# FFN gates turned and broadcast as twelve bf16 rows instead of four fp32 rows, and register waits bounded by an AND

## The reference

```python
all_out = _experts_mlp(x, eW1, eb1, eW2, eb2, eW3, eb3)      # 4 experts, 256 -> 128 -> 64 -> 256
shared = _shared_mlp(x, sW1, sb1, sW2, sb2, sW3, sb3)
gates = jax.nn.softmax(x @ gW + gb, axis=-1)
topv, topi = jax.lax.top_k(gates, TOPK)                      # the best 2 of 4
topw = jax.nn.softmax(topv, axis=-1)
sel = jnp.take_along_axis(all_out, topi[:, :, None, :], axis=-1)
gated = jnp.sum(sel * topw[:, :, None, :], axis=-1)
return shared + gated
```

## Time and profile before

| | us |
|---|---|
| median of three runs | 1826.44 |
| lowest and highest of them | 1825.96, 1827.35 |
| span of the profiled execution, first to last instruction | 1822.0 |
| median less that span | 4.4 |
| TensorE busy, of the span | 1704.3 |
| VectorE, ScalarE, GpSimd busy | 942.9, 569.8, 186.2 |

### The profile page before, as it was taken

How to read it: one execution, slowest core, us unless ns; L and a number is a source line. 1 busy time by engine, 2 the same in 40 slices (tenths; PEclk the granted TensorE clock), 3 DMA queues, 4 the chain that set the end, 5 groups by cost and what they waited for, 6 DMA issues and landing times.

```text
span 1822.0 us, 30852 instructions
## 1 busy us (share of the span) xinstructions
PE 1704.3 (94%) x10162; PEld 1363.7 (75%) x10163; DVE 942.9 (52%) x1593; ACT 569.8 (31%) x854; POOL 186.2 (10%) x260
## 2 busy tenths in 40 slices
PE   6999999888879999999999999999999999998995
PEld 4898988888766777777777777767677777787784
DVE  7999999998862300111144443552312243245436
ACT  2135677888880100000011111343400000004442
POOL 4000000000000100000000000000000000153683
PEclk9999999999999999999999999999999999999998
DMA  4203344544569445454443435900054434434375
GB/s 98 1 34 124 146 175 192 206 201 200 228 239 356 132 139 154 134 161 149 138 127 110 127 124 149 232 1 0 15 187 167 141 110 120 151 117 132 106 241 183
DMA packets 136919, 261.73 MB, mean 144 GB/s; under 512 B 22236, under 2 KB 74735, under 8 KB 136606
## 3 DMA queue, kind: packets, MB, share of 16 engines
q1 hardware_dynamic: 116824, 237.02, 40.2%
q0 software_dynamic: 5808, 14.70, 2.2%
q10 hardware_dynamic: 14230, 9.29, 1.7%
HBM read 161.13 MB, written 108.09 MB: 148 GB/s over the span
## 4 chain that ended last, share of the span: by engine, by line
issue 55%; PE 27%; ACT 6%; DVE 4%; ACTq 3%; DMA 2%; POOL 1%; DVEq 1%; SPq 0%; POOLq 0%
PE ps L2112 12%; PE ps L2113 4%; PE ps L2143 3%; ACT wide L870 3%; ACTq L914 2%; PE ps L2363 2%; ACT ps L818 2%; PE ps L2347 2%; DVE act_c L1373 1%; PE ps L2355 1%; PE ps L2339 1%; PE ps L2160 0%; ACTq L859 0%; DMA count_matrix<-wide 0%; PE ps L2015 0%
## 5 line engine op out<-in xcount | busy, mean ns | idle before, releaser
L2143 PE MATMUL ps<-wide 128*128 128x320 f32 (+1 forms) x2000 | 533.2, 427 | 0.0
L2143 PEld LDWEIGHTS ps<-wide 128*128 128x128 f32 x2000 | 378.4, 190 | 141.3 <-issue 0.4
L2112 PE MATMUL ps<-early,act_c 128*128 128x200 bf16 x2400 | 295.7, 252 | 43.4 <-issue 18.7
L2143 PE MATMUL ps<-wide,act_a 128*128 128x320 f32 (+1 forms) x1000 | 264.4, 426 | 2.3 <-DMA wide<-weight_matrix 2.2
L2112 PEld LDWEIGHTS ps<-early,act_c 128*128 128x128 bf16 x2400 | 220.5, 97 | 58.1 <-issue 57.3
L2143 PEld LDWEIGHTS ps<-wide,act_a 128*128 128x128 f32 x1000 | 189.8, 190 | 75.4 <-DMA wide<-weight_matrix 2.4
L870 ACT COPY wide<-ps 128x832 f32<-128x832 f32 x200 | 169.8, 849 | 121.8 <-PE ps L2113 120.6
L818 ACT ACTIVATE ps<-wide 128x832 f32 (+1 forms) x200 | 173.4, 868 | 42.0 <-ACT wide L870 33.7
L1373 DVE TENSOR_TENSOR act_c<-act_a,pair_tab 128x3072 bf16<-128x3072 bf16 x98 | 169.1, 1750 | 14.6 <-PE ps L2113 14.6
L1501 DVE TENSOR_TENSOR wide<-ps,rows 128x1280 f32<-128x1280 f32 x10 | 14.9, 1491 | 283.5 <-PE ps L2160 283.5
L2112 PE MATMUL ps<-act_a,act_c 128*128 128x200 bf16 x1152 | 140.3, 251 | 11.0 <-ACT ps L818 4.2
(11 more groups left out here) (261 smaller groups left out, 1808.5 us busy)
## 6 DMA issues: line engine op xcount, KB each, us to landing
wide<-weight_matrix SPq DMA_DIRECT2D x90, 800.0 KB, 4.5
wide<-count_matrix SPq DMA_DIRECT2D x45, 800.0 KB, 4.6
weight_matrix<-wide SPq DMA_DIRECT2D x60, 480.0 KB, 2.5
count_matrix<-wide SPq DMA_DIRECT2D x60, 480.0 KB, 2.6
weight_matrix<-wide SPq DMA_DIRECT2D x20, 560.0 KB, 2.7
count_matrix<-wide SPq DMA_DIRECT2D x20, 560.0 KB, 2.7
wide<-weight_matrix SPq DMA_DIRECT2D x20, 400.0 KB, 3.7
routed_tokens<-in_x_dram SPq DMA_DIRECT2D x2, 3072.0 KB, 30.4
```

The costliest lines, as they stand in the source:

```text
L2112: nc.tensor.matmul(weights, hot_parts[:, slot % PART_SLOTS, part, two, :, k], hot_key[mask_slot][:, mask_two, 0:WCOLS, k], start=False, st ...
L2143: i = nc.tensor.matmul(ps[:, 2 * sub + h, 0:n], features[:, q * QUADS + t, h * P:(h + 1) * P], moving, start=q == 0 and t == 0, stop=q == ...
```

## The change

The gates of a block are split into three bf16 parts whose sum is the fp32 value: the value rounded to bf16, the rest rounded to bf16, and the rest of that. The three parts of the four gates are twelve columns, so that turning them gives twelve rows, and `sel` has three ones in each column, which add the parts up again in fp32 in PSUM. The matmuls of both steps have bf16 operands. At a split VectorE has three copies and two subtractions with a drain before each, where it had a drain and one copy. GpSimd builds a bf16 identity and three diagonals of `sel` instead of one.

Beside this, the waits against a register in the accumulation (TensorE's `acc_free`, ScalarE's `pair_done`) now take the register's value ANDed with 2047. The values are all smaller than that, so nothing changes in what is waited for.

```diff
-        sel = sb("sel", [EXPERTS, PAIRS, P])
+        ident_half = sb("ident_half", [P, P], BF16)
+        sel = sb("sel", [GATE_ROWS, PAIRS, P], BF16)
-        ffn_gates_here = small[:, 360:360 + SUPER * EXPERTS].rearrange("p (t e) -> p t e", t=SUPER)
+        ffn_gate_parts = small[:, 360:360 + SUPER * GATE_ROWS // 2].bitcast(BF16).rearrange("p (t r) -> p t r", t=SUPER)
+        ffn_gate_left = small[:, 284:284 + SUPER * EXPERTS].rearrange("p (t e) -> p t e", t=SUPER)
-        gate_t = act_c_flat0[0:EXPERTS, 5760:5760 + SCOLS]
+        gate_t = act_c_flat0[0:GATE_ROWS, 5760:5760 + SCOLS // 2].bitcast(BF16)
...
-                    act.wait_ge(pair_done, end)
+                    act.wait_ge(pair_done, act.scalar_reg_alu(ALU.bitwise_and, end, COUNTED))
...
-                act.copy(gate_t[0:EXPERTS, :], ps[0:EXPERTS, 3:5, :].rearrange("p b c -> p (b c)")[:, 0:SCOLS]).then_inc(gate_rows_done, 1)
+                act.copy(gate_t, ps[0:GATE_ROWS, 3:5, :].rearrange("p b c -> p (b c)")[:, 0:SCOLS]).then_inc(gate_rows_done, 1)
...
+            pool.tensor_copy(ident_half[:, :], ident[:, :]).then_inc(pool_chain, 1)
             pool.memset(sel[:, :, :], 0.0).then_inc(pool_chain, 1)
-            pool.wait_ge(pool_chain, count(1))
+            pool.wait_ge(pool_chain, count(2))
             picks = sel[:, :, :].rearrange("e q (h m) -> e q h m", h=2)
-            pool.affine_select(out=picks, in_=picks, compare_op=ALU.not_equal, fill=1.0, base=0,
-                               pattern=[[-2, PAIRS], [-1, 2], [0, EH2]], channel_multiplier=1).then_inc(routing_consts, 1)
+            for j in range(GATE_PARTS):
+                part_ready, n = (routing_consts, 0) if j == GATE_PARTS - 1 else (pool_chain, 1)
+                pool.affine_select(out=picks, in_=picks, compare_op=ALU.not_equal, fill=1.0, base=-j * EXPERTS,
+                                   pattern=[[-2, PAIRS], [-1, 2], [0, EH2]], channel_multiplier=1).then_inc(part_ready, 1)
+                pool.wait_ge(pool_chain, count(n))
...
-            dve.drain()
-            dve.tensor_copy(ffn_gates_here, ffn_gate[:, 0:SUPER, :]).then_inc(ffn_gates_copied, 1)
+            def split_gates(s):
+                gates = ffn_gate[:, here(s), :]
+                for j in range(GATE_PARTS):
+                    part = ffn_gate_parts[:, :, j * EXPERTS:(j + 1) * EXPERTS]
+                    dve.drain()
+                    i = dve.tensor_copy(part, gates)
+                    if j < GATE_PARTS - 1:
+                        dve.drain()
+                        dve.tensor_tensor(ffn_gate_left, gates, part, ALU.subtract)
+                        gates = ffn_gate_left
+                i.then_inc(ffn_gates_copied, 1)
+
+            split_gates(0)
             second_layer(SUPERS - 1)
...
             def next_gates(s):
-                dve.drain()
-                dve.tensor_copy(ffn_gates_here, ffn_gate[:, here(s + 1), :]).then_inc(ffn_gates_copied, 1)
+                split_gates(s + 1)
...
-                            pe.wait_ge(acc_free, nc.s_assert_within(free, 1, WINDOWS // GROUP, skip_runtime_bounds_check_because="a group's number plus one"))
+                            pe.wait_ge(acc_free, pe.scalar_reg_alu(ALU.bitwise_and, free, COUNTED))
...
             def gate_rows_of(s):
                 pe.wait_ge(ffn_gates_copied, s + 1)
+                pe.wait_ge(routing_consts, 1)
                 for t in range(SUPER):
-                    i = nc.tensor.matmul(block_t_ps(3, t)[0:EXPERTS, :], ffn_gates_here[:, t, :], ident[:, :], start=True, stop=True)
+                    i = nc.tensor.matmul(block_t_ps(3, t)[0:GATE_ROWS, :], ffn_gate_parts[:, t, :], ident_half[:, :], start=True, stop=True)
                 i.then_inc(gate_rows_ready, 1)
```

More of the change, by code:

```diff
@@ L75 @@
 UNROLL = MASK_SLOTS * MASK_BATCHES
+COUNTED = 2047
 BATCHES = -(-STEPS_P // MASK_PAIRS) * MASK_BATCHES
@@ L99 @@
 PASSES = 3
+GATE_PARTS = 3
+GATE_ROWS = GATE_PARTS * EXPERTS
 STEPS = (1, 5, 4)
```

## The result

| | us |
|---|---|
| before, measured with it, median of five (lowest, highest) | 1825.96 (1823.74, 1827.35) |
| changed kernel, median of five (lowest, highest) | 1832.06 (1830.5, 1838.81) |
| ratio | 1.0046, 95% interval 1.003 to 1.0062 |
| profiled execution of the changed kernel, and its span | 1830.5, 1828.7 |

So 0.46% slower, where 0.3% faster was forecast, and outside the range. The changed kernel's own time is 1.8 us above its span, not the 4.4 that I had set for before from the difference of two executions.

The account below looks back on a forecast made before the run. TensorE, busy 94% of the span, was taken as the bound, its queue being on the path at line starts. Gates -10.75, split +1.0 and ANDs +4.2 gave -5.55 us: 1826.44 to 1820.9 us, range 1815.5 to 1827.

Parts of the forecast that it names:

- gate rows and broadcasts in bf16: FFN on TensorE: shorter matmuls save 10.75 us over five blocks, with bounds 9.5 to 12.
- first split: Ahead of the last second layer: four more VectorE instructions, not hidden, cost 1.0 us, bounds 0.6 to 1.4.
- ANDs: Accumulation: ANDs before the waits cost 4.1 us on TensorE and 0.1 on ScalarE, 4.2 together.
- clock: The sum had no term for the clock; more frequent falls were left to the third rival.
- The step that failed: Accumulation: three of a line's four ANDs cost nothing, as TensorE's queue takes 0.26 us a pair against the array's 0.36.
- The first AND: Start of each line: exposed after the load, 0.09 us on 45 lines, 4.1 us.
- the price of a step: TensorE's queue: a register instruction costs its 32 ns and a step, 0.06 to 0.12 us, taken as 0.09.
- The count of lines: Accumulation: 74 lines times TensorE's share of the chain, 0.61, gave 45 lines that pay for an AND.
- the wait of block 1: FFN: TensorE's wait for VectorE's gated biases grows from 1.43 to 3.1 us, so block 1 saves only 0.9 us.
- the later splits: FFN, after block 0's gates and later: hidden in VectorE's waits for TensorE, with 1.2 us or more to spare.
- third rival: Clock falls more often through longer waits; up to 1.7 us a stretch, two more give 1824.3 us; chance 0.15.
- Rival 2: Line start gets much dearer: four ANDs together or costlier register results, +16 us, kernel at 1832.9 us; chance 0.1.

Follow-up runs that it names:

- e14: Changed kernel with acc_free waits every eight pairs in the first 54 lines only and the first split behind the last second layer: 1827.00 us, ratio 0.9988.
- e16: Kernel before (fp32 gates) with the ANDs and the thinned waits of e14: 1837.94 us, ratio 1.005.
- e13: The changed kernel itself, measured again in rounds with before at 1829.93 us: 1827.88 us, ratio 1.0002.
- e9: Changed kernel with a wait for acc_free every eight pairs instead of every four, so two ANDs a line instead of four: ratio 1.0001.
- e6: Changed kernel with two more ANDs ahead of each of a line's later three waits, six more a line: ratio 1.0185.
- e11: Changed kernel with the first split of the gates moved behind the last second layer: ratio 0.9999.
- the last group: e13 to e16, measured on one chip in the same rounds as before, whose median there was 1829.93 us.
- e15: e14 with matmuls of no use filling TensorE's waits for VectorE in the FFN: 1826.21 us, ratio 0.998.
- e7: Changed kernel with three more ANDs ahead of the first wait of each line, directly behind the load: ratio 1.0099.
- e5: Changed kernel with the ANDs written, for two of three lines, between the last four pairs of the line before: ratio 1.0034.
- e1: Kernel before with unsigned 16-bit tables in place of 32-bit ones, ScalarE's too: 2276.69 us, ratio 1.2258.
- e10: e9 with the two unread numbers left out of the table, 18 values a line in place of 20: 2057 us, ratio 1.1055.

## Why the prediction was wrong, step by step

| term | forecast | measured |
|---|---|---|
| gate rows and broadcasts in bf16 | -10.75 | -10.5 to -11.4 (e14 against e16) |
| first split | +1.0 | +1.0 |
| ANDs | +4.2 | +10.2 |
| clock | 0 | about +7 in the profiled pair; none between the means of before and e13 |

**The step that failed** is "Three of the four ANDs of a line lie where the queue is ahead of the array: nothing". The first AND was right (0.09 forecast, 0.10 measured), and so was the price of a step. But at a line's end the queue runs on into the next load, and whatever it is behind there comes out as idle time of the array, just like what stands behind the load: the queue's lead fell from 1.26 to 1.17 us. The queue has time to spare only once it waits for the array, and before the change it did so over the last two pairs of a line, some 0.2 us. Of the 0.28 us that three ANDs take, about 0.17 were covered and 0.11 came through, for which the prediction had nothing; e9, which removes two, gives 0.09 back, and e6, which adds six, has no cover left at all. The spacing of 0.26 against 0.36 us was true and told only that the queue catches up, not that it had caught up in time for the load.

**The count of lines** was low too. I weighted 74 lines with TensorE's share of the chain and got 45; the delay grows over 52 to 54 lines, about evenly, and then stops. VectorE's gapless time up to 330 us absorbed nothing: after the change it is busy for 277.4 of the 283 us. 52 lines x 0.206 us are the 10.7 us: some 5 of them are the first AND, forecast at 4.1, and more than 5 the later three, forecast at nothing.

**The FFN** came as costed: durations of 0.37 us, 2.5 to 2.6 us in each undisturbed block, the wait of block 1 at 3.47 us, the later splits hidden. e14 against e16 gives 10.5 to 11.4 for a forecast of 10.75. What I charged at the first split was right to 0.1 us, and e11 takes it back at that place.

**The clock** was my third rival, with 3.4 us and 0.15. In the profiled pair it took more: 10.2 us more at half clock in the FFN, which is 5.1 us if it costs half its length (an estimate), and two stretches of 3.4 us at 555 and 958 us that before had not, with 0.6 and 1.7 us. The 1.7 us that the prediction takes for one stretch is so shown once. In the sum for the pair, 10.2 + 0.6 + 1.7 + 1.0 + 5.1 - 11.9 = 6.7 us, the 11.9 for the FFN is only what is left for it, so it is no check of the other terms. But that the *change* makes the clock fall more often isn't shown, and the last group speaks against it: the mean granted clock is 0.9859 over 31 executions of before and 0.9858 over 12 of e13. Ten profiles with bf16 gates and no fills had 3.4 to 20.5 us at half clock between 1150 us (or the same place in the slower kernels) and the end of the FFN, five with fp32 gates 10.2 to 23.9. The fall at 1210.5 us follows 3.4 us in which TensorE was busy 3.03, the one at 1244.6 follows 1.17, and filling the waits did not end them. That a longer wait brings more falls was the prediction's guess. The second fall would agree, as it lies in the idle 3.47 us of block 1; the first does not, nor does e15's first, which follows 3.40 us of TensorE without a gap. What picks the stretches stays open.

Rival 2 named the right direction and the wrong mechanism: the ANDs stand at their waits, one each, and none is dearer than 0.1 us. That its 1832.9 us lies close to the measured 1832.06 is chance, as it took 16 us for the ANDs where 10.2 were found, and the rest is the clock's or open. It had put its point of decision at 0.22 us a line, for 45 lines; the 0.206 us found, over more lines, are 10.7 us, where the FFN gives back 9.75. By the terms without the clock the change is a draw, which e13 shows (1830.6 against 1830.8 us at equal clock); in the first measurement it was 0.46% slower.

## What to carry to other kernels

In this kernel TensorE's queue loads its registers once a line, and its slack was one sum for the whole line, some 0.2 us, on which each AND in the line drew with 0.09 us. To price such an instruction in another queue that loads once a round, look at the end of the round for steps in which the queue waits for the array: here the last two (0.352 and 0.358 us against 0.244) were what the line absorbed. The spacing in the middle, 0.244 us, told only that the queue was catching up.

A change of a few tenths of a per cent is smaller than what lay between executions of one kernel: 0.6% over 31 of before, from 1823.80 us at a mean granted clock of 0.989 to 1835.15 at 0.982. Give the granted clock beside each time, and don't explain a difference from one pair of profiles. With five executions of each, two kernels can differ in it by chance. The two kernels that beat before (e14 by 0.12%, barely clear of the noise, and e15 by 0.2%) keep the bf16 gates, hide the split and halve the waits where TensorE sets the pace.

## What the runs showed of the hardware

- An AND, a record of 32 to 36 ns, took 0.091 to 0.097 us of TensorE's queue wherever it was measured (0.092 and 0.091 us by the delay of e6 and e7, 0.093 to 0.097 from its record to the next, in medians).
- TensorE's queue issued a pair's instructions in 0.244 us and then waited for the array over the last two pairs of a line (0.352 and 0.358 us): work added to the line was hidden up to about that much and no further.
- TensorE's TENSOR_LOAD took at the least 1.10, 1.36 and 1.61 us for 16, 20 and 24 values of 32 bits (e5), so 0.063 us a value. With 16-bit values it took 4.7 us or more for 20 (e1), and with lines 72 bytes apart every other one took 4.3 us or more (e10).
- Executions of one kernel differed in their mean granted clock, from 0.989 to 0.982 in 31 of before, and 0.001 of it went with 1.14 us of 1830 in the five kernels of the last group.
- In e5 the ANDs were executed at the waits that use their values (296 ALU_OP records on the line of the wait, L2125, the one at 118.1 us directly behind a load), although the program's text has them, for two of three lines of the table, between the last four pairs of the line before.
